# A decoder layer on one core: weights and context laid out by the host, MLP weights quantised in pieces inside the early slots

## The reference

```python
x = x + self_attention(layernorm(x))          # W_attn, per-head layernorm of q and k, causal softmax, W_proj
x = x + cross_attention(layernorm(x), ctx)    # Wq, Wk, Wv; top_k(scores, 32), softmax over those, Wo
x = x + mlp(layernorm(x))

def _weight_quant(w):                          # w_gate, w_up: (2048, 512); w_down: (512, 2048)
    scale = 1.0 / jnp.clip(jnp.mean(jnp.abs(w)), 1e-05)
    return jnp.clip(jnp.round(w * scale), -1.0, 1.0) / scale
def _bitlinear(x, w): return einsum(_act_quant(x), _weight_quant(w))
mlp(x) = _bitlinear(silu(_bitlinear(x, w_gate)) * _bitlinear(x, w_up), w_down)
```

## Time and profile before

| what | value |
|---|---|
| median of 3 runs | 3911.12 us (3903.92 to 3913.15) |
| profiled execution | 3917.24 us, its span 3915.5 us |
| mean granted PE clock | 0.867 of full |
| busy PE / DVE / ACT / POOL | 3310.2 / 3220.0 / 2451.7 / 1917.9 us |
| preparation (until the pipeline's first DMA) | 0 to 136.36 us |
| slots with self attention alone | 136.36 to about 517 us |

### The profile page before, as it was taken

How to read it: one execution, slowest core, us unless ns; L and a number is a source line. 1 busy time by engine, 2 the same in 40 slices (tenths; PEclk the granted TensorE clock), 3 DMA queues, 4 the chain that set the end, 5 groups by cost and what they waited for, 6 DMA issues and landing times.

```text
span 3915.5 us, 61337 instructions
## 1 busy us (share of the span) xinstructions
PE 3310.2 (85%) x18502; PEld 2433.7 (62%) x18502; DVE 3220.0 (82%) x7571; ACT 2451.7 (63%) x4921; POOL 1917.9 (49%) x2444
## 2 busy tenths in 40 slices
PE   1577888999989998999999989999899988877765
PEld 1355567766666676667667667667666766554542
DVE  4311189999989999899989998999989998999961
ACT  2344466676777677667766677767666776555533
POOL 0122334446555466546654655546554654355445
PEclk7677878898999989988989999988998898887768
DMA  8112232232223222322223222322233221211100
GB/s 279 46 49 65 80 84 73 74 82 75 51 76 88 75 69 79 84 79 74 76 72 84 75 52 74 87 76 67 79 88 83 65 71 41 62 46 36 33 22 19
DMA packets 167443, 283.04 MB, mean 72 GB/s; under 512 B 40639, under 2 KB 52939, under 8 KB 166606
## 3 DMA queue, kind: packets, MB, share of 16 engines
q1 hardware_dynamic: 160782, 275.98, 25.9%
q10 hardware_dynamic: 6336, 3.15, 0.3%
HBM read 113.27 MB, written 31.46 MB: 37 GB/s over the span
## 4 chain that ended last, share of the span: by engine, by line
DVE 33%; PE 32%; POOL 11%; issue 8%; ACT 6%; SPq 4%; DMA 1%; DVEq 0%; POOLq 0%; ACTq 0%
DVE cW L881 15%; DVE top L876 12%; PE bank L682 6%; PE bank L607 6%; PE bank L654 5%; SPq L513 4%; PE bank L593 3%; PE bank L670 2%; PE bank L701 2%; PE bank L635 2%; POOL hh L1111 2%; POOL srs L1147 2%; POOL hh L1115 2%; PE bank L694 2%; DVE smx L1013 2%
## 5 line engine op out<-in xcount | busy, mean ns | idle before, releaser
L881 DVE MATCH_REPLACE8 cW<-top,cW 128x512 f32<-128x512 f32 x1536 | 1026.3, 676 | 0.0
L876 DVE MAX8 top<-cW 128x8 f32<-128x512 f32 x1536 | 980.7, 680 | 0.0
L1168 POOL TENSOR_TENSOR cS<-cS,cW 128x512 f32<-128x512 f32 x512 | 642.2, 1276 | 233.2 <-ACT cW L825 232.7
L797 ACT ACTIVATE PT<-bank 128x512 f32<-128x512 f32 (+3 forms) x1024 | 538.0, 525 | 314.4 <-PE bank L593 310.6
L607 PE MATMUL bank<-cv,PT 128*128 128x33 f32 x4096 | 586.0, 290 | 121.8 <-ACT PT L797 120.6
L607 PEld LDWEIGHTS bank<-cv,PT 128*128 128x128 f32 x4096 | 555.0, 210 | 157.0 <-ACT PT L797 151.0
L1175 POOL TENSOR_SCALAR cnb<-top 128x2 f32<-128x2 f32 x256 | 49.3, 193 | 871.6 <-DVE top L876 857.9
L607 PEld LDWEIGHTS bank<-sv,PT 128*128 128x128 f32 x2560 | 398.7, 211 | 77.7 <-ACT PT L797 55.4
L825 ACT ACTIVATE cW<-cW,cnb 128x512 f32<-128x512 f32 x512 | 347.8, 734 | 127.6 <-DVE cW L881 127.2
L819 ACT ACTIVATE cS<-cS,cnb 128x512 f32<-128x512 f32 x512 | 380.1, 742 | 46.9 <-POOL cnb L1175 24.0
L682 PE MATMUL bank<-w_group,xT 128*128 128x384 f32 x1024 | 403.3, 541 | 0.0
(11 more groups left out here) (151 smaller groups left out, 6131.8 us busy)
## 6 DMA issues: line engine op xcount, KB each, us to landing
sk_stack<-part SPq DMA_DIRECT2D x512, 64.0 KB, 2.0
sq_stack<-part SPq DMA_DIRECT2D x512, 64.0 KB, 2.0
ck_stack<-part SPq DMA_DIRECT2D x512, 64.0 KB, 2.0
cq_stack<-part SPq DMA_DIRECT2D x512, 64.0 KB, 2.0
w_group<-wa_by_group SPq DMA_DIRECT2D x32, 768.0 KB, 4.8
w_group<-wc_by_group SPq DMA_DIRECT2D x32, 768.0 KB, 4.3
feed<-in_x SPq DMA_DIRECT2D x32, 256.0 KB, 3.0
feed<-in_ctx SPq DMA_DIRECT2D x32, 256.0 KB, 3.0
```

Source lines behind the costliest of these rows:

```text
L797: act.activation(PT[k][:, 0:n], turned_ps[k][:, 0:n], ACT.Copy).then_inc(turned_read, step("turned_read", label))
L876: dve.max(top8[:, j, r, :], src[:]).then_inc(topk, step("topk", (c, r, "max", j)))
L881: dve.match_replace(cW[j][:], top8[:, j, r, :], src[:], REPLACED).then_inc(topk, step("topk", (c, r, "replace", j)))
L1168: pool.tensor_tensor(cS[m % 2][j][:], cS[m % 2][j][:], cW[j][:], ALU.subtract).then_inc(cprob, step("cprob", (m, j)))
```

## The change

The host gives the arrays in the order in which the kernel wants them: the context transposed (`ctx_t`), `W_attn` by head group (`wa`), the cross weights transposed and by group (`wc`), `W_proj`, `Wo` and the MLP weights transposed in 16 pieces of 128x512 each (`mlp`), biases as 128 rows of 32 (`bias`), scale columns (`gcol`, `ccol`). The arithmetic on weights stays on the chip. `setup` and both its blocks are gone; what they did moves into the pipeline block:

- Centring: `centre(g)` on DVE, at the end of slots -5, -1, 3 and 7, on the group that lies in `w_group`; SP stores the result to `wa_by_group` (slots -4, 0, 4, 8) for the later batches. The first load of `w_group` is at slot -7.
- Quantising matrix k = 0, 1, 2 (gate, up, down): 16 loads from slots -7, -3, 4 (four a slot); `weight_sums` on DVE at the end of slots -4, 2, 8 and of the slot after each; a PE unit `wsum` of one column in cell 0 of slots -2, 4, 10; `weight_quant` on DVE after `norms` in slots -1, 5, 11 and the two after each (6, 5 and 5 pieces); `convert` on ACT ahead of cells 2 to 7 of the same slots. The pieces lie in tiles of the later cross and MLP work: `cS`, `cW`, `co` for k = 0 and 2; `x1T`, `hh`, `ctxT`, `th`, `uc`, `x2t`, `x2res` for k = 1.
- `prologue` on DVE: the ones columns, and the bias split on 128 partitions. SP gathers it to `bias16` by nine DMAs.
- Context: one DMA of 1 MB a batch into `ctxT` (slot 9, then 30, 46, ...), no feed units.
- New waits: `self_qkv` of the first four groups on `centred`, the first on `bias_in`; the unit two after `wsum` on `wq_scale`; the first MLP units and the first cross `match_replace` on all 48 conversions.

```diff
+PIECES = 16
+W_LOAD, W_ABS, W_SUM, W_QUANT = (-7, -3, 4), (-4, 2, 8), (-2, 4, 10), (-1, 5, 11)
+QUANT_PARTS = (range(0, 6), range(6, 11), range(11, 16))
+CTX_FIRST = 9
...
-    ctx = {15: (0, 1), 16: (2, 3)}
...
+    u[0] += [("wsum", k) for k in range(3) if W_SUM[k] == s]
...
-        setup(nc, dict(W_attn=W_attn, b_attn=b_attn, wa_dram=wa_dram, wc_dram=wc_dram, banks=banks,
...
-            loads = [(max(FIRST, at), which, g, last_use[uses[k - 1][1]](uses[k - 1][2]) if k else None)
+            loads = [(at if k else FIRST, which, g, last_use[uses[k - 1][1]](uses[k - 1][2]) if k else None)
...
+                        if stored:
+                            sp.wait_ge(wa_out, 16 * stored)
+                        src = wc_in[g % NG] if which == "cross" else wa_in[g] if g < NG else wa_dram[g % NG]
...
+                        if s % NT == 0 and 0 <= s // NT + 1 < NG:
+                            g = s // NT + 1
+                            sp.wait_ge(centred, g + 1)
+                            sp.dma_start(wa_dram[g], w_group[:].rearrange("p c (k n) -> p c k n", k=3)).then_inc(wa_out, 16)
...
+                        for k in range(3):
+                            if 0 <= s - W_LOAD[k] < 4:
+                                if k == 2 and s == W_LOAD[k]:
+                                    sp.wait_ge(wq_done, PIECES)
+                                for i in range(4 * (s - W_LOAD[k]), 4 * (s - W_LOAD[k]) + 4):
+                                    sp.dma_start(staged[k][i], mlp_in[k, :, i, :]).then_inc(wq_in[k][i // 8], 16)
...
+                        if s == CTX_FIRST:
+                            sp.wait_ge(wq_done, 2 * PIECES)
+                            sp.dma_start(ctxT[:], ctx_t[0]).then_inc(ctx_in, 16)
...
+                    def convert(s, i):
+                        for k in range(3):
+                            if 0 <= s - W_QUANT[k] < 3 and i < len(QUANT_PARTS[s - W_QUANT[k]]):
+                                piece = QUANT_PARTS[s - W_QUANT[k]][i]
+                                act.wait_ge(wq_q, PIECES * k + piece + 1)
+                                act.activation(quantised[k][piece], staged[k][piece], ACT.Copy, bias=-MAGIC,
+                                               saturate=False).then_inc(wq_done, 1)
...
+                    def centre(g):
+                        w = w_group[:, :, 0:2 * P].rearrange("p c (h d) -> p c h d", d=HD)
+                        dve.wait_ge(w_in, upto("w_in", ("self", g), 16))
+                        dve.tensor_reduce(hmean[:], w, AXX, ALU.add).then_inc(head_mean, 1)
+                        dve.tensor_scalar(hmean[:], hmean[:], 1.0 / HD, None, ALU.mult).then_inc(head_mean, 1)
+                        dve.tensor_tensor(w, w, hmean[:].unsqueeze(3).to_broadcast([P, NC, 2 * HG, HD]), ALU.subtract).then_inc(
...
+                    def weight_quant(s):
+                            if 0 <= s - W_QUANT[k] < 3:
+                                pieces = QUANT_PARTS[s - W_QUANT[k]]
+                                dve.wait_ge(wq_scale, 2 * k + 2)
+                                for i in pieces:
+                                    w = staged[k][i]
+                                    dve.tensor_scalar(w, w, winv[:, k:k + 1], 1.0, ALU.mult, ALU.min).then_inc(wq_clip, 1)
+                                for i in pieces:
+                                    w = staged[k][i]
+                                    dve.wait_ge(wq_clip, PIECES * k + i + 1)
+                                    dve.tensor_scalar(w, w, -1.0, MAGIC, ALU.max, ALU.add).then_inc(wq_q, 1)
```

More of the change, by code:

```diff
@@ L77, in feeds @@
 def feeds(s):
-    x = {-6: (0, 1, 2), -4: (3,)}
-    ctx = {15: (0, 1), 16: (2, 3)}
     out = []
-    for src, table in (("x", x), ("ctx", ctx)):
-        for at, tiles in table.items():
-            b, rest = divmod(s - at, SLOTS)
-            if rest == 0 and 0 <= b < NB:
-                out += [(src, NT * b + t) for t in tiles]
+    for at, tiles in ((-6, (0, 1, 2)), (-4, (3,))):
+        b, rest = divmod(s - at, SLOTS)
+        if rest == 0 and 0 <= b < NB:
+            out += [("x", NT * b + t) for t in tiles]
     return out
@@ L380, in pipeline @@
             ring = {f: n for n, f in enumerate(fs)}
-            normed = [f for f in fs if f[0] == "x"]
+            normed = fs
             for f in fs:
@@ L641, in unit @@
                         kind = u[0]
-                        if kind == "cross_oT":
+                        if kind == "wsum":
+                            pe.wait_ge(wq_sum, u[1] + 1)
+                            mm = pe.matmul(ps[:, 0:1], ones32[:], wsum3[:, u[1]:u[1] + 1], start=True, stop=True)
+                        elif kind == "cross_oT":
                             pe.wait_ge(co_norm, upto("co_norm", SLOTS * (u[1] // NT) + SLOTS - NT + u[1] % NT))
@@ new lines, in weight_sums @@
+                    def weight_sums(s):
+                        for k in range(3):
+                            half = s - W_ABS[k]
+                            if half not in (0, 1):
+                                continue
+                            dve.wait_ge(wq_in[k][half], 8 * 16)
+                            for i in range(8 * half, 8 * half + 8):
+                                dve.tensor_reduce(wsums[:, i:i + 1], staged[k][i], AXX, ALU.add,
+                                                  apply_absolute_value=True).then_inc(wq_abs, 1)
+                            if half == 1:
+                                dve.wait_ge(wq_abs, PIECES * (k + 1))
+                                dve.tensor_reduce(wsum3[:, k:k + 1], wsums[:], AXX, ALU.add).then_inc(wq_sum, 1)
@@ L1454 @@
+NAMES = ["x", "ctx_t", "wa", "wc", "wproj", "wo", "mlp", "bias", "gcol", "ccol"]
 def kernel(**inputs):
```

369 lines of the change are left out of this document (132 added, 237 removed).

## The result

The changed kernel takes 3787.93 us (median of 4 executions, 3774.83 to 3791.17), beside 3907.52 us for the kernel before in the same session (4 executions, 3891.5 to 3913.15): a ratio of 0.9696, 95% interval 0.9663 to 0.9729. The forecast was 3785. The profiled execution took 3774.83 us, 10 us under the mean of all nine executions of this kernel (3784.5); that of before, 3917.24, lay 8 us above the mean of its own (3908.9). So the two traces differ by 142 us where the kernels differ by 124, and I compare the traces by places in the pipeline, not by their ends. Of all executions in this document one is left out: one of the kernel with the short pause, further down, took 7325.6 us, nearly twice the time of its others.

The account below looks back on a forecast made before the run. Preparation bound by itself, early self-attention slots by a loop through PE, POOL and SP, later slots by DVE and PE together. 3917.2 - 129.8 + 13 - 9 = 3791.4, less 6.1 for a median: 3785 us, range 3755 to 3838.

Parts of the forecast that it names:

- The start: Preparation ahead of the pipeline goes; first projection near 23.5 us against 153.27, gain 129.8 us, bounds 121 to 136.
- The slots: Centring and quantising inside slots with self attention alone: 13 us added, mostly hidden in waits, bounds -5 to 105.
- I count nothing for them: ACT's 48 weight conversions, 29 us of work standing ahead of cells in the early slots, were priced at zero.
- the maximum of slot 5: Sign: behind twelve clips on DVE, the row maximum would be about 1 us late.
- The context: 32 feeds with PE transposes and ACT copies go: 0.3 us for each of 28, 9 us gained, bounds 0 to 34.
- It costs nothing: The new 1 MB context load in SP's queue, waiting until slot 30 and needed in slot 33, was priced at zero.
- the 395 to 405 that I named: Sign: the first full cross slot, at 517 us before, should start at 395 to 405 us.
- The correction to the median: The profiled execution of 3917.24 us is 6.1 above the median 3911.12, so 3791.4 became 3785 us.
- In a line: Clips, sums and conversions stop the early slots' loop each time: 105 us in place of 13, 3877 us; chance 0.08.
- More is won: Start as short as before, all context feeds count at 15 us, slots cost 3: 3764 us; chance 0.09.
- rival 4: PE's granted clock falls, in slots with self attention alone (3916 us) or from 517 us on (3947); chance 0.03.
- rival 2: DVE's clips and POOL's power block each other in nine visits, 49 us in place of 9: 3825 us; chance 0.12.

Follow-up runs that it names:

- the short pause: Changed kernel with VectorE filling eight 128x512 tiles with zeros ahead of everything while SP waits, a delay of 4.3 us: 3795.38 us.
- the second trace: Profiled execution from timing the changed kernel again with no edit: 3783.52 us, ratio 0.9678.
- pieces-late run: Changed kernel with the first eight weight pieces issued behind the fourth x tile in SP's queue: 3783.56 us, ratio 0.9683.
- the run with the feeds last: Kernel before, with the feeds' loads issued behind the store and reload of the x tile in SP's queue: 3905.92 us, ratio 0.9994.

## Why the prediction was right, point by point

**The start** (129.8 forecast, 129.9 measured). The chain was right in every link: split done near 4.3 (5.3 forecast), nine DMAs at 0.63 us (0.62), end of them 10.0 (11), the fourth tile's statistics from 19.6 (20), first projection 23.33 (23.5). The pieces were issued at 0.49 us each, not 0.35, 1.2 us more for eight; the tile landed when I said all the same, because the split had ended 1 us early. That the sum agrees to a tenth is luck: the second trace has 24.19, a gain of 129.1. The pieces-late run shows that the eight pieces ahead of the fourth tile are 6.8 us of the start.

**The slots** (13 forecast, 10.5 measured, bounds -5 to 105). The size was right and the split wrong. I gave all 13 us to DVE's visits with clips and sums and nothing to ACT's conversions or the centrings. The run without clips and sums shows 3.5 us for the former and 7.1 for all the rest. The step that failed is "I count nothing for them": in slot 5 `so` to `so` grew by 1.4 us with and without clips. The prediction also expected the maximum of slot 5 to be 1 us late and `snb` of slot 6 on time; they were 0.5 and 0.3 us late.

**The context** (-9 forecast). The whole difference at the end, 124 us, less 129.9 and 10.5, leaves about -5 for it, and 5.7 us of gain stand between the marks of slots 15 and 17. The mechanism of the forecast, transposes off a shared bound, fits the 2.5 us at each of five seams (transposes and ACT's copies were not separated), but in the kernel before the total moved by 3 us with an error of 2; the failed step is counting 0.3 us for each feed as if each were on the path, where those at slots 47 and 48 cost 2.5 us from the mark of slot 48 on and nothing before it (27.9 and 27.8 us from mark 47 to 48). And "It costs nothing", said of SP's queue, looked at the new load only. What went from that queue mattered more at the mark of slot 17: the feeds ahead of a store, found by the run with the feeds last, and a stretch of low clock behind them that was in no term of mine. As a result the first full cross slot came at 391.5, ahead of the 395 to 405 that I named. The rest should have been 9 us shorter: the two profiled executions have 17 us, but the means leave nothing, 124 us at the end against 125.5 gained by then.

**The sum.** Errors of 2.5 us (slots) and 4 us (context) of opposite sign cancelled, which is luck too. The correction to the median was right in kind: the profiled execution of before is a long one.

**The rivals.** In a line (3877): the measured 3788 and the run without clips exclude it. More is won (3764): no, the start was as long as forecast. The clock: 0.74 and 0.90 are unchanged, so rival 4 has nothing (the 6.8 us near slot 17 don't show in such means). The clips and POOL's power, rival 2: twelve clips ran inside one power with no block, so its 49 us are absent. Yet what is behind it is there at three other places: the subtraction that takes 2.87 us, POOL's scaling that takes 1.66, and one of POOL's `part` operations, which takes 3.07 where the median of its line is 1.27. The clips themselves never stretched. By line, instructions of the changed kernel (duration ns min/median/max):

```profile
L1105 DVE TENSOR_TENSOR w_group<-w_group,hmean x4: 1226/1226/2873, 21.9 to 169.8; 128x1024 f32<-128x1024 f32 x4
```
```profile
L1136 DVE TENSOR_SCALAR cS<-cS,winv x16: 473/478/485, 42.6 to 239.0; 128x512 f32<-128x512 f32 x16
```
```profile
L1295 POOL TENSOR_TENSOR part<-part x14: 1257/1270/3068, 53.2 to 375.2; 128x512 fp32r<-128x512 f32 x14
```

The subtraction begins 0.11 us behind POOL's scaling of 1.91 us and is 1.65 us longer than alone, nearly the 1.80 that the scaling had left. The `part` operation begins at 53.17 among clips that end at 55.11, and is 1.80 us longer; without clips it isn't. POOL's scaling of 128x512 begins 0.21 us behind a subtraction that has 1.02 us left, and is 0.89 us longer; with the subtraction out of the way it isn't. So in three pairs one engine waited out the other, whichever had begun first, and in the pair that I priced, clips and power, neither did: both ran for over 4 us together, and the power was longer by only 0.25 to 0.29 us (5.43 in the run without clips too).

The Trainium skill (SBUF — State Buffer, "SBUF: two separate sides") says that a DVE instruction in a two-port mode, or one with two SBUF inputs against a GpSimd instruction that reads SBUF, excludes the GpSimd instruction and is excluded by it, for the whole length of the one that starts first; my prediction used only the first half of that. The trace agrees at three places, 1.65, 0.89 and 1.80 us, and not for the power, 5.68 us beside twelve clips.

## What to carry to other kernels

Look for stages in which the bounding engines idle on a loop, and put one-off work there: 70 us of DVE work cost 3.5 us. Count each added instruction on each engine of that loop, ACT's above all if its instructions stand ahead of the copies that everyone waits for. When DMAs are taken out of a queue, look at what was issued behind them, and at the granted clock where PE waited for it: 2.2 us at a reload were 5.2 at the next mark. And compare marks inside the program, not two single totals, before a difference of some us gets a mechanism: here one execution scatters by 5 to 6 us around its mean. A line through many runs needs the same care: look whether both halves of it say the same.

## What the hardware showed that was not expected

- POOL's power of 128x32 takes 5.43 us alone and 5.68 to 5.72 beside DVE's clips, which don't slow. Other pairs run one behind the other: a multiplication of 128x1024 on POOL and then a subtraction of 128x1024 on DVE (1.65 us lost), that subtraction and then a scaling of 128x512 on POOL (0.89), clips and a POOL operation of 128x512 begun among them (1.80), once each in this program.
- Eight projection matmuls (128x384) took 2.85 us at a granted clock of 1.00 and 5.49 at 0.50; the stretch at 0.50 lasted 6.8 us and stood at a wait of 2.84 us.
- A fill of 128x512 takes 0.48 to 0.53 us on DVE.
- From slot 21 to 149 the ten traces of kernels without context feeds show 3239.5 to 3263.4 us, the four with feeds 3256.4 to 3267.0, and two executions of one kernel 3239.5 and 3244.4.
